# A Mamba layer with experts on one Trainium2 core: a ring of sixteen state halves, sums two steps later, and two products moved to GpSimd

## The chip, the core and the metric

The kernel runs on one core of a Trainium2 chip. TensorE multiplies matrices, VectorE (DVE) runs the scan, ScalarE (ACT) the exponentials and copies, GpSimd (POOL) elementwise products and indirect DMAs, SyncE (SP) issues the other DMAs. Each engine takes its instructions in the order of its own program; semaphores tie them together. The metric is the device time of one execution in microseconds.

## The reference

The input x has 8 batches of 512 tokens with 128 features. It is normalised; on the result work a bidirectional Mamba block and a layer of 8 experts, and both are added to x. All is float32. For each direction of Mamba (256 channels, 16 states each):

```
xi    = silu(conv4(x @ in_w.T) + conv_b)        z = x @ in_w.T (second half)
dt, B, C = split(xi @ x_w.T)                     # 8, 16, 16
delta = softplus(dt @ dt_w.T + dt_b)             A = -exp(A_log)
h[t]  = h[t-1] * exp(delta[t] * A) + delta[t] * xi[t] * B[t]
y[t]  = sum over the states of h[t] * C[t]       # per channel
out   = ((y + xi * D) * silu(z)) @ out_w.T
```

The backward direction runs over the reversed sequence. Both outputs are joined and go through combine_w; the residual is added. The experts choose one of 8 by the largest router logit for each token and compute `down(silu(gate) * up)`.

## The kernel before

A **unit** is one batch in one direction; there are 16 (two per batch, forward even, backward odd). A unit's 256 channels times 16 states are laid out as 16 **steps** of a state half of 128 partitions x 1024 numbers (32 channels x 4 groups of states on the partitions, 2 states x 512 times in the free dimension). So there are 256 steps of the scan and 32 **half batches** i of eight steps each (the two halves of a unit's channels). All five engine programs are loops over the same step number m (`for m in range(STEPS)`), and each engine does at step m, in the order in which its loop lists them, what the functions `fronts`, `tiles_at`, `gathers`, `out_step` and so on put there.

For a step m of the scan:
- TensorE spreads delta*u over the partitions (`spread_du`, L589, tile in_b), one matmul for a pair of steps, in the odd step before it;
- VectorE multiplies it by B (`du_B`, L1131), two steps at once in the even step; ScalarE makes the decay exp(delta*A) (`decay`, L947, tile dA, ring of 4), two steps ahead, from delta_rep, which SyncE copies from tmpA (`load_pair`);
- VectorE scans (`scan`, L1148 forward, L1150 backward) into hs, in the odd step; hs is a ring of NH = 13 state halves;
- GpSimd multiplies hs by C in place (L1360); for the steps in `C_ON_DVE` = 41, 56, 180, 217, 226, 255 VectorE does it (`times_C`, L1157);
- TensorE sums the states into bank Y (`sum_states`, L623): for half batch i the even halves at step 8i+12, the odd halves at 8i+13, each a set of eight matmuls that waits for the last product of its four steps. A scan that reuses a half waits for the sum that read it.

After half batch i: Y is copied to yg (`next_y`, L930, ScalarE) and multiplied by silu(z) (the **gate**, L1343, GpSimd) at step 8i+14; half batches 3, 4, 5 and 31 have their gate on VectorE (L1168). TensorE opens Y for the next half batch with xi*D (`skip`, L614) at step 8i+8. The projection out of a batch (`out_mm`, L667) waits for the gates; it runs in bank F, on top of the bias (`bias_mm`, L635) and the residual (`residual_mm`, L642), at step 32b+42 to 32b+44 for all batches but the last.

The front part of the next units (in projection, x and dt projection, softplus) is woven in between. GpSimd makes delta and delta*u of a unit (`delta_du`, L1302 and L1307) some seven steps before it starts. Bank F passes from one user to the next: `bias_mm` waits for the copy of z of unit 2b+3 (`keep_z`, L882, ScalarE), and that copy, which overwrites zs, waits for the gate of the same buffer two units earlier (`wait_gated`, half batch 2(v-2)+h).

From step 33 on GpSimd also scatters the tokens to their experts by indirect DMA (L1371, 32 of them), from step 208 on it gathers the experts' results (L1333, L1336, four at a time, in steps 208, 212 and so on up to 236); in a step's program they stand ahead of the gate. The experts run between on TensorE and ScalarE.

Of the kernel before, what the change touches and what calls it, by code (L numbers as in the profile page):

```python
# [21 lines left out]
NSTEP = J * R // RH  # L22
UNITS = 2 * NB
# [3 lines left out]
EPS = 1e-5  # L27
LAST = UNITS * NSTEP
NP, NR = 3, 5
NA, NH = 4, 13  # L30
LEAD = 2
LATE = 2
CLEAR = 3
# [2 lines left out]
NW, ND = 2, 2  # L36
SILU_SET, EXP_SET = "silu_and_others", "natural_log_exp_and_others"
GATE_ON_DVE = (3, 4, 5, 2 * UNITS - 1)
C_ON_DVE = (41, 56, 180, 217, 226, LAST - 1)

C_ID, C_TRI, C_SEL, C_IOTA, C_THR, C_NOTFIRST, C_TILE = 0, 128, 256, 288, 296, 328, 584
C_SPREAD = C_TILE + NTILE
# [55 lines left out]
def out_step(b, k):  # L98


    s0 = NSTEP * (2 * b + 1)
    if b < NB - 1:
        return s0 + NSTEP + (12, 12, 12, 12, 10, 13, 13, 12)[k]
    return s0 + (8, 9, 17, 21, 4, 22, 25, 17)[k]


STEPS = max(LAST + 6, out_step(NB - 1, 6) + 1, gather_step(NB - 1) + 10)
# [25 lines left out]
def mamba_moe_kernel(nc, x, in_wT, conv_wT, x_wT, dt_wT, A_log, out_w, comb_wT, comb_b,  # L133
                     col_vectors, router_wT, gate_up, down, consts, out):
    ctx = ExitStack()
    with ctx:
# [365 lines left out]
        def tensor_program(e):  # L502
# [192 lines left out]
            for m in range(STEPS):  # L695
                u, s = divmod(m, NSTEP)
                for i in range(1, 2 * UNITS):
                    if 8 * i + 8 == m:
                        skip(i)
                if m == 0:  # L700
                    z_proj(0, 0)
# [9 lines left out]
                    in_proj(v, 1, 0)  # L711
                for v in fronts(m, -13, -13):
                    in_proj(v, 1, 1)
                if m >= 12 and m - 12 < LAST - 8 and (m - 12) % 8 == 0:
                    u2, s2 = divmod(m - 12, NSTEP)
                    sum_states(u2, s2 // 8, 0)
                for v in fronts(m, -10, -11):
                    x_proj(v)
                for b in turns(m, -18):
# [40 lines left out]
                for b in gathers(m, 7):  # L760
                    if b < NB - LATE:
                        final_mm(b)
                if m >= 13 and m - 13 < LAST - 8 and (m - 13) % 8 == 0:
                    u2, s2 = divmod(m - 13, NSTEP)
                    sum_states(u2, s2 // 8, 1)
                for b in range(NB):
                    if out_step(b, 4) == m:
                        bias_mm(b)
# [36 lines left out]
        def scalar_program(e):  # L805
# [118 lines left out]
            def next_y(i):  # L924

                u, h = divmod(i, 2)
                e.wait_ge(pe_y, 2 * i + 2)
                if u >= 2:
                    e.wait_ge(pe_out, i - 3)
                e.copy(yg[:, u % 2, h, :], Y[:, :]).then_inc(act_y, 1)  # L930
# [55 lines left out]
            for m in range(STEPS):  # L986
# [75 lines left out]
                for v in fronts(m, -8, -9):  # L1062
                    table(EXP_SET)
                    softplus(v, 0)
                if m % 8 == 6 and m >= 8:
                    if m // 8 - 1 not in GATE_ON_DVE:
                        next_y(m // 8 - 1)
                for b in range(NB):
                    if out_step(b, 5) == m:
                        e.wait_ge(pe_out, 4 * b + 4)  # L1070
# [16 lines left out]
        def vector_program(e):  # L1087
# [191 lines left out]
            for m in range(STEPS):  # L1279
                u, s = divmod(m, NSTEP)  # L1280
                for i in GATE_ON_DVE:
                    if m == (LAST + 5 if i == 2 * UNITS - 1 else 8 * i + 15):
                        gate(i)
                for i in range(2):
                    if m >= R0:
                        route(2 * (m - R0) + i)
                    if m < LAST and m % 2 == 0:
                        du_B(m + i)
                    elif m < LAST:
                        scan(m - 1 + i)  # L1290
                for x in C_ON_DVE:
                    if m % 2 and x in (m - 1, m):
                        times_C(x)
# [3 lines left out]
        def gpsimd_program(e):  # L1297
# [17 lines left out]
            for m in range(STEPS):  # L1315
                u, s = divmod(m, NSTEP)
                for b in gathers(m, 2):
                    i = b - (NB - LATE)
                    if b == 0:
                        e.wait_ge(out_ys[0], 16 * (NTILE + 1) // 2)  # L1320
                        e.wait_ge(out_ys[1], 16 * (NTILE // 2))
                    if i < 0:
                        if b >= 2:
                            e.wait_ge(pe_fin, b - 1)
                    elif i == 0:
                        e.wait_ge(out_xn, 16 * NB)
                        e.wait_ge(pe_xn_turned, NB)
                    else:
                        e.wait_ge(out_fin[0], 16 * (NB - LATE) // 2)
                    for k in range(KB):  # L1330
                        at = bass.IndirectOffsetOnAxis(ap=pos_u[:, b * KB + k:b * KB + k + 1], axis=0)
                        if i < 0:
                            e.indirect_dma_start(out=rows_of(b)[:, k, :], out_offset=None, in_=ffn_d,  # L1333
                                                 in_offset=at).then_inc(in_gather[b % 2], 16)
                        else:
                            e.indirect_dma_start(out=late_in[i][:, k, :], out_offset=None, in_=ffn_d,  # L1336
                                                 in_offset=at).then_inc(in_late[i], 16)
                if m % 8 == 6 and m >= 8 and m // 8 - 1 not in GATE_ON_DVE:
                    i = m // 8 - 1
                    k = (slice(None), i // 2 % 2, i % 2, slice(None))  # L1340
                    e.wait_ge(act_y, gates_on_pool(i))
                    e.wait_ge(act_zs, i + 1)
                    e.tensor_tensor(yg[k], yg[k], zs[k], ALU.mult).then_inc(pool_gated, 1)  # L1343
                for n in [n - 1 for n in tiles_at(m, 11) if n % 2] + gates_at(m, 12):
                    e.wait_ge(act_up, n + 1)
                    if n == NTILE - 1:
                        e.wait_ge(act_gate, NTILE)
                    else:
                        e.wait_ge(act_thf, n // 2 * 2 + 2)
                    e.tensor_tensor(th_f[:, n % 3, :], th_f[:, n % 3, :], up_f[:, n % 2, :],  # L1350
                                    ALU.mult).then_inc(pool_acted, 1)
                for h in range(2):
                    for v in fronts(m, (-7, -4)[h], (-8, -6)[h]):
                        delta_du(v, h)
                if m < LAST and m not in C_ON_DVE:
                    p, rh, jj = place(s)
                    e.wait_ge(dve_scan, m + 1)
                    if s == 0:
                        wait_bc(e, u)
                    e.tensor_tensor(hs[:, m % NH, :], hs[:, m % NH, :],  # L1360
                                    C_rep[:, u % 2, RH * rh:RH * rh + RH, :].rearrange("p r t -> p (r t)"),
                                    ALU.mult).then_inc(pool_C, 1)
                for c in range(NB):
                    for k in range(KB):
                        if R0 + 6 + (20 * c + 5 * k) // 8 == m:
                            if k == 0:
                                e.wait_ge(in_sort[c % 2], 16 * (c // 2 + 1))
                            if c == 0 and k == 0:
                                e.wait_ge(dve_route, N_POS)
                                e.wait_ge(out_clear, 160)  # L1370
                            e.indirect_dma_start(  # L1371
                                out=sorted_d, out_offset=bass.IndirectOffsetOnAxis(
                                    ap=pos_u[:, c * KB + k:c * KB + k + 1], axis=0),
                                in_=attn_in[:, c % 2, k, :], in_offset=None).then_inc(out_sort[c % 2], 16)
# [71 lines left out]
```

## Time and profile before

| | |
|---|---|
| median of 3 runs | 923.8 us (922.23 to 923.9) |
| span of the profiled execution | 921.1 us, 2.7 less than the median |
| VectorE busy | 882.0 us, 96% |
| GpSimd busy | 801.1 us, 87% |
| TensorE matmuls busy | 736.6 us, 80% |
| ScalarE busy | 699.8 us, 76% |
| products with C on GpSimd | 250, 585.5 us |
| scans | 256, 570.4 us |

A span runs from the first to the last instruction of the profile. A row of a timeline has the start, the duration, the engine, the line, the operation, out<-in and, in brackets, the idle time before it with what ended it. Durations of one instruction in a group are means in ns. Neighbouring instructions of an engine overlap by some 0.1 us at their ends.

### The profile page before, as it was taken

What the parts mean: (1) busy time and instruction counts of PE and PEld (TensorE: products, weight loads), DVE (VectorE), ACT (ScalarE), POOL (GpSimd) and SP (SyncE); (2) the same over time, 40 slices, a digit from 0 to 9 for tenths busy, and PEclk for the clock granted to TensorE, in tenths of its full rate; (3) what the DMA queues carried; (4) which work ended last, traced back from release to release, by engine and by line L of the source; (5) the groups of instructions that cost most, each with busy time, mean ns of one, the idle gap of its engine ahead of it and who ended that gap; (6) DMA issues with size and microseconds to landing.
All of it is one profiled execution on the core that took longest, in us unless ns stands there. A gap on an engine that the chain in (4) does not pass through costs nothing. (4 is left out here: it accounts for less than half of the span.)

```text
span 921.1 us, 10735 instructions
## 1 busy us (share of the span) xinstructions
PE 736.6 (80%) x3033; PEld 327.7 (36%) x3033; DVE 882.0 (96%) x631; ACT 699.8 (76%) x1183; POOL 801.1 (87%) x450
## 2 busy tenths in 40 slices
PE   8678877777488978979788987979786987878377
PEld 5233322231134534444343534436332431323022
DVE  5899999999899999999999999999999999999986
ACT  5798876646569789888989889998979776585531
POOL 1578786999999989998799898999798989999994
PEclk9978789788698999999999999989999799879578
DMA  7875342343265546445365636455554345553300
GB/s 229 224 221 144 109 111 58 139 100 101 110 162 158 152 154 175 138 136 149 134 151 177 156 84 209 124 185 125 181 140 134 85 95 163 108 170 75 85 0 12
DMA packets 87227, 123.45 MB, mean 134 GB/s; under 512 B 7929, under 2 KB 58490, under 8 KB 83202
## 3 DMA queue, kind: packets, MB, share of 16 engines
q1 hardware_dynamic: 85122, 118.58, 46.5%
q0 software_dynamic: 2048, 4.20, 1.5%
q8 instruction: 25, 0.41, 0.2%
q14 instruction: 32, 0.26, 0.1%
HBM read 75.44 MB, written 14.29 MB: 97 GB/s over the span
## 5 line engine op out<-in xcount | busy, mean ns | idle before, releaser
L1360 POOL TENSOR_TENSOR hs<-hs,C_rep 128x1024 f32<-128x1024 f32 x250 | 585.5, 2362 | 52.1 <-DVE hs L1150 27.8
L947 ACT ACTIVATE dA<-delta_rep,A_sb 128x511 f32<-128x511 f32 x512 | 338.2, 717 | 92.8 <-DVE hs L1150 47.1
L1131 DVE TENSOR_TENSOR in_b<-in_b,B_rep 128x1024 f32<-128x1024 f32 x256 | 300.1, 1216 | 15.7 <-PE in_b L589 14.7
L1150 DVE TENSOR_TENSOR_SCAN hs<-dA,in_b 128x1024 f32<-128x1024 f32 x128 | 285.3, 2267 | 5.3 <-PE y L623 5.3
L1148 DVE TENSOR_TENSOR_SCAN hs<-dA,in_b 128x1024 f32<-128x1024 f32 x128 | 285.1, 2267 | 1.4 <-PE y L623 1.4
L589 PE MATMUL in_b<-du,cst 128*128 128x512 f32 x256 | 160.8, 714 | 57.3 <-DVE hs L1150 43.6
L623 PE MATMUL y<-hs,cst 128*32 128x512 f32 x1024 | 139.5, 652 | 21.9 <-POOL hs L1360 21.9
L550 PE MATMUL front<-xpad,w_in 128*128 128x512 f32 x248 | 119.3, 616 | 9.0 <-ACT xi L876 7.3
L956 ACT ACT_TABLE_LOAD x71 | 91.1, 1283 | 8.3 <-PE moe L733 3.7
L589 PEld LDWEIGHTS in_b<-du,cst 128*128 128x128 f32 x256 | 46.8, 214 | 134.4 <-issue 132.6
L623 PEld LDWEIGHTS y<-hs,cst 128*32 128x32 f32 x1024 | 29.6, 116 | 113.8 <-issue 71.0
L550 PEld LDWEIGHTS front<-xpad,w_in 128*128 128x128 f32 x248 | 46.3, 197 | 66.0 <-issue 48.3
L582 PE MATMUL front<-tmpB,w_dt 8*128 8x512 f32 x62 | 40.1, 730 | 25.5 <-ACT tmpB L909 16.7
L564 PE MATMUL front<-xpad,w_in 128*128 128x512 f32 x62 | 38.8, 711 | 15.9 <-ACT tmpB L912 8.6
L1302 POOL TENSOR_TENSOR tmpA<-tmpA,tmpB 128x512 f32<-128x512 f32 x31 | 39.5, 1276 | 12.9 <-ACT tmpB L922 12.8
L733 PEld LDWEIGHTS moe<-xsT,gu_w 128*128 128x128 f32 x234 | 32.7, 202 | 35.2 <-issue 35.2
L614 PE MATMUL y<-xi,diag_D 128*128 128x512 f32 x62 | 39.4, 723 | 5.3 <-ACT yg L930 4.3
L1343 POOL TENSOR_TENSOR yg<-yg,zs 128x512 f32<-128x512 f32 x28 | 35.6, 1270 | 9.1 <-ACT yg L930 9.1
L751 PEld LDWEIGHTS moe<-dn_w,th_f 128*128 128x128 f32 x234 | 33.7, 205 | 26.9 <-issue 18.4
L733 PE MATMUL moe<-xsT,gu_w 128*128 128x128 f32 x234 | 35.7, 291 | 9.4 <-ACT ys L1019 5.6
L1307 POOL TENSOR_TENSOR du<-tmpA,xi 128x512 f32<-128x512 f32 x31 | 39.5, 1273 | 2.4
L1371 POOL DMA_INDIRECT sorted_tokens<-attn_in,pos_u x32 | 33.4, 1045 | 8.9 <-issue 8.8
(147 smaller groups left out, 803.0 us busy)
## 6 DMA issues: line engine op xcount, KB each, us to landing
delta_rep<-tmpA SPq DMA_DIRECT2D x126, 256.0 KB, 3.9
C_rep<-dbc_scratch SPq DMA_DIRECT2D x16, 1024.0 KB, 7.2
B_rep<-dbc_scratch SPq DMA_DIRECT2D x15, 1024.0 KB, 5.0
gu_w<-in_gate_up SPq DMA_DIRECT2D x39, 384.0 KB, 3.8
dn_w<-in_down SPq DMA_DIRECT2D x39, 192.0 KB, 2.6
xs<-sorted_tokens SPq DMA_DIRECT2D x39, 64.0 KB, 3.9
sorted_ffn<-ys SPq DMA_DIRECT2D x39, 64.0 KB, 2.4
sorted_tokens<-up_f SPq DMA_DIRECT2D x9, 256.0 KB, 4.5
```

Source lines behind the costliest of these rows:

```text
L550: i = e.matmul((M if v == 0 and h else F)[:, :], w_in[:, d, k, h * P:(h + 1) * P], xpad[:, at:at + L], start=(k == 0), stop=(k == NTAP - 1))
L582: e.matmul((M if v == 0 and h else F)[:, :], w_dt[:, d, h * P:(h + 1) * P], dbc[0:DR, :], start=True, stop=True).then_inc(pe_dt, 1)
L589: e.matmul(in_b[:, 2 + 2 * (j % 2), :], spread(j), du[:, du_slot(v, j // 4), :], start=True, stop=True).then_inc(pe_du, 1)
L623: i = e.matmul(Y[c * DD:(c + 1) * DD, :], sel, hs[:, (m + 2 * c + rh) % NH, r * L:(r + 1) * L], start=False, stop=(rh == 1 and r == RH - 1 ...
L733: i = e.matmul(M[:, c * P:(c + 1) * P], gu_w[:, w, 0, c * P:(c + 1) * P], xsT[:, n % 2, :], start=True, stop=True)
L947: i = e.activation(dA[:, m % NA, r * L + 1:(r + 1) * L], src, ACT.Exp, scale=A_sb[:, d, 2 * p + jj, RH * rh + r:RH * rh + r + 1])
L956: e.preload_act_table_set(name)
L1131: e.tensor_tensor(to, in_b[:, 2 + 2 * odd, :].unsqueeze(1).broadcast_to([P, RH, L]), by, ALU.mult).then_inc(dve_mult, 1)
L1148: e.tensor_tensor_scan(to, a[:, 0:n], b, 0.0, ALU.mult, ALU.add).then_inc(dve_scan, 1)
L1150: e.tensor_tensor_scan(to[:, ::-1], a[:, 1:n + 1][:, ::-1], b[:, ::-1], 0.0, ALU.mult, ALU.add).then_inc(dve_scan, 1)
L1302: e.tensor_tensor(tmpA[:, h, :], tmpA[:, h, :], tmpB[:, h, :], ALU.add).then_inc(pool_delta, 1)
L1360: e.tensor_tensor(hs[:, m % NH, :], hs[:, m % NH, :], C_rep[:, u % 2, RH * rh:RH * rh + RH, :].rearrange("p r t -> p (r t)"), ALU.mult).th ...
```

## The change

Six edits. The ring hs has 16 state halves, made possible by a smaller scratch for the descriptors of GpSimd's DMAs, 4096 bytes of each partition. The sums of half batch i are at step 8i+14 and 8i+15 (for the half batch 30 at 8i+12 and 8i+13 as before). The copy of Y and the gate on GpSimd are at step 8i+16, on VectorE at 8i+17 (half batch 31 as before). skip of half batch i is at 8i+10, of half batch 31 as before. The products with C of steps 41 and 56 are on GpSimd. The steps of all other work stay.

```
-NA, NH = 4, 13
+NA, NH = 4, 16
-C_ON_DVE = (41, 56, 180, 217, 226, LAST - 1)
+C_ON_DVE = (180, 217, 226, LAST - 1)
+def sum_step(i, rh):
+    return 8 * i + rh + (14 if i < 2 * UNITS - 2 else 12)
+def y_step(i):
+    return sum_step(i, 0) + 2
+def skip_step(i):
+    return y_step(i - 1) + 2
+def halves_at(step, m):
+    return [i for i in range(2 * UNITS - 1) if step(i) == m]
 # TensorE
-                    if 8 * i + 8 == m:
+                    if skip_step(i) == m:
                         skip(i)
-                if m >= 12 and m - 12 < LAST - 8 and (m - 12) % 8 == 0:
-                    u2, s2 = divmod(m - 12, NSTEP)
-                    sum_states(u2, s2 // 8, 0)
+                for i in range(2 * UNITS - 1):
+                    if sum_step(i, 0) == m:
+                        sum_states(i // 2, i % 2, 0)
 # (the odd halves, at m - 13, in the same way with sum_step(i, 1))
 # ScalarE
-                if m % 8 == 6 and m >= 8:
-                    if m // 8 - 1 not in GATE_ON_DVE:
-                        next_y(m // 8 - 1)
+                for i in halves_at(y_step, m):
+                    if i not in GATE_ON_DVE:
+                        next_y(i)
 # VectorE
-                    if m == (LAST + 5 if i == 2 * UNITS - 1 else 8 * i + 15):
+                    if m == (LAST + 5 if i == 2 * UNITS - 1 else y_step(i) + 1):
                         gate(i)
 # GpSimd
-                if m % 8 == 6 and m >= 8 and m // 8 - 1 not in GATE_ON_DVE:
-                    i = m // 8 - 1
+                for i in halves_at(y_step, m):
+                    if i in GATE_ON_DVE:
+                        continue
-    nc = bacc.Bacc("TRN2", target_bir_lowering=False, num_devices=1)
+    nc = bacc.Bacc("TRN2", target_bir_lowering=False, num_devices=1,
+                   dynamic_dma_scratch_size=4096)
```

## Rows read from the trace of the kernel before

**Rows 1.** Busy time by stretch; columns: stretch, length, engines with counts, TensorE clock, DMA share.

```profile
157.00:326.00 169.00, 131.56 (x507) 54.59 (x511) 164.08 (x101) 116.48 (x197) 161.17 (x96) 0.85 0.45 127
326.00:744.00 418.00, 354.23 (x1680) 175.78 (x1670) 414.79 (x252) 369.82 (x634) 382.63 (x207) 0.95 0.53 147
744.00:897.00 153.00, 109.33 (x364) 37.86 (x362) 146.50 (x90) 94.11 (x146) 143.46 (x88) 0.83 0.38 99
```

**Rows 2.** Costliest groups, VectorE: busy us, mean ns of one, idle before with releaser.

```profile
L1131 DVE TENSOR_TENSOR in_b<-in_b,B_rep 128x1024 f32<-128x1024 f32 x256 | 300.1, 1216 | 15.7 <-PE in_b L589 14.7 <-DMA B_rep<-dbc_scratch 0.8
L1157 DVE TENSOR_TENSOR hs<-hs,C_rep 128x1024 f32<-128x1024 f32 x6 | 9.2, 1530 | 0.1
```

**Rows 3.** Costliest groups, GpSimd.

```profile
L1360 POOL TENSOR_TENSOR hs<-hs,C_rep 128x1024 f32<-128x1024 f32 x250 | 585.5, 2362 | 52.1 <-DVE hs L1150 27.8 <-DVE hs L1148 23.5
```

**Rows 4.** Timeline of VectorE, its products with C of steps 41 and 56.

```profile
179.04 3.05 DVE L1157 TENSOR_TENSOR hs<-hs,C_rep 128x1024 f32<-128x1024 f32 x1
...
236.17 1.19 DVE L1157 TENSOR_TENSOR hs<-hs,C_rep 128x1024 f32<-128x1024 f32 x1
```

**Rows 5.** Timeline of GpSimd beside these two, and delta of unit 4.

```profile
181.16 1.81 POOL L1371 DMA_INDIRECT sorted_tokens<-attn_in,pos_u  x1 [0.17 <-issue]
...
236.39 1.84 POOL L1371 DMA_INDIRECT sorted_tokens<-attn_in,pos_u  x1 [0.17 <-issue]
238.54 0.96 POOL L1371 DMA_INDIRECT sorted_tokens<-attn_in,pos_u  x1 [0.30 <-issue]
...
249.99 1.26 POOL L1302 TENSOR_TENSOR tmpA<-tmpA,tmpB 128x512 f32<-128x512 f32 x1
```

**Rows 6.** Timeline of TensorE, steps 60 to 76 (x counts weight loads too).

```profile
247.78 3.64 PE L623 MATMUL y<-hs,cst 128*32 128x512 f32 x16 [10.30 <-POOL hs L1360]
...
294.36 1.71 PE L635 MATMUL front<-comb_bias,ones 1*128 1x512 f32 x2
...
299.70 2.83 PE L623 MATMUL y<-hs,cst 128*32 128x512 f32 x16
```

**Rows 7.** Timeline of VectorE, steps 61 to 64, and step 78.

```profile
251.49 2.29 DVE L1150 TENSOR_TENSOR_SCAN hs<-dA,in_b 128x1024 f32<-128x1024 f32 x1 [3.05 <-PE y L623]
253.69 2.34 DVE L1131 TENSOR_TENSOR in_b<-in_b,B_rep 128x1024 f32<-128x1024 f32 x2
...
260.31 2.33 DVE L1131 TENSOR_TENSOR in_b<-in_b,B_rep 128x1024 f32<-128x1024 f32 x2
...
308.54 2.36 DVE L1131 TENSOR_TENSOR in_b<-in_b,B_rep 128x1024 f32<-128x1024 f32 x2 [1.83 <-PE in_b L589]
```

**Rows 8.** Timeline of ScalarE, the decay of step 64.

```profile
256.27 1.33 ACT L947 ACTIVATE dA<-delta_rep,A_sb 128x511 f32<-128x511 f32 x2 [10.91 <-DMA delta_rep<-tmpA]
```

**Rows 9.** Timeline of GpSimd, delta of unit 5 at step 72.

```profile
294.22 1.28 POOL L1302 TENSOR_TENSOR tmpA<-tmpA,tmpB 128x512 f32<-128x512 f32 x1
```

**Rows 10.** Waits of VectorE between 326 and 744 us: total us, times, longest.

```profile
DVE in_b L1131 <- PE in_b L589: 2.7, 3, 1.3
DVE hs L1148 <- PE y L623: 0.5, 2, 0.3
```

**Rows 11.** Timeline of GpSimd, gates of half batches 24 and 27, delta of unit 15.

```profile
739.67 1.26 POOL L1343 TENSOR_TENSOR yg<-yg,zs 128x512 f32<-128x512 f32 x1 [0.60 <-ACT yg L930]
...
830.97 1.26 POOL L1343 TENSOR_TENSOR yg<-yg,zs 128x512 f32<-128x512 f32 x1
...
841.75 1.28 POOL L1302 TENSOR_TENSOR tmpA<-tmpA,tmpB 128x512 f32<-128x512 f32 x1
```

**Rows 12.** Timeline of ScalarE, the copy of z of unit 15.

```profile
832.32 0.59 ACT L882 COPY zs<-front 128x512 f32<-128x512 f32 x1 [1.56 <-POOL yg L1343]
```

**Rows 13.** Timeline of TensorE, steps 234 to 237.

```profile
832.95 1.12 PE L635 MATMUL front<-comb_bias,ones 1*128 1x512 f32 x2 [2.39 <-ACT zs L882]
...
837.62 1.92 PE L623 MATMUL y<-hs,cst 128*32 128x512 f32 x16
...
840.43 3.73 PE L667 MATMUL front<-w_out,yg 128*128 128x128 f32 x32
844.00 1.02 PE L589 MATMUL in_b<-du,cst 128*128 128x512 f32 x2
```

**Rows 14.** Timeline of VectorE, step 246.

```profile
878.65 2.37 DVE L1131 TENSOR_TENSOR in_b<-in_b,B_rep 128x1024 f32<-128x1024 f32 x2 [3.35 <-PE in_b L589]
```

More of the change, by code:

```diff
@@ L762, in tensor_program @@
                         final_mm(b)
-                if m >= 13 and m - 13 < LAST - 8 and (m - 13) % 8 == 0:
-                    u2, s2 = divmod(m - 13, NSTEP)
-                    sum_states(u2, s2 // 8, 1)
+                for i in range(2 * UNITS - 1):
+                    if sum_step(i, 1) == m:
+                        sum_states(i // 2, i % 2, 1)
                 for b in range(NB):
```

## The prediction

> **What bounds the kernel now.** I read four views, in this order: busy time by stretch, the costliest groups of each engine, the timelines of the engines around every idle piece of VectorE, and who waited for whom. The first shows three stretches after the routing has begun: VectorE is busy for 164.1 of 169 us, 414.8 of 418 and 146.5 of 153 [rows 1]. So the scan of VectorE is the bound, and all it can still give is its idle time and what is taken off it. But GpSimd is nearly as full in the first and third stretch (161.2 of 169, 143.5 of 153), while in the second it idles for 35.4 us. VectorE's own waits for TensorE's in_b come to 14.7 us in the whole run, and its six products with C to 9.2 [rows 2]. One of its products with C takes 2362 ns [rows 3], and a pair of steps on VectorE has a period of 260.31 - 253.69 = 6.62 us [rows 7], so GpSimd falls behind when scatters, gathers or gates come on top. Most of VectorE's longer stalls come from that lag.
>
> I number steps as the code does (step m, state half m, i the half batch of eight steps). By counting, the scan at 251.49 is that of step 61, the products of VectorE at 179.04 and 236.17 are those of steps 41 and 56.
>
> **1. Two products leave VectorE (steps 41, 56).** They took 3.05 and 1.19 us there [rows 4]: 4.24 us, all on VectorE's own path. On GpSimd they cost 2 x 2.36 = 4.72 us [rows 3]. Beside each of them an indirect DMA of GpSimd took 1.81 and 1.84 us, with 0.96 for its undisturbed neighbour [rows 5]; I take these 2 x 0.86 = 1.7 us back, so GpSimd is 3.0 us later from step 57 on (bounds: 3.0 and 4.7). [...]
>
> **2. Sixteen halves and sums two steps later.** The scan of step 61 stood 3.05 us until the sum of half batch 6 was done, after a TensorE wait of 10.30 us for GpSimd [rows 6, 7]. With the new ring, the scan may run ten steps ahead of the product instead of seven, so this stall goes. Together with part 1 VectorE would be 4.24 + 3.05 = 7.3 us earlier at step 64. What is late next is also on GpSimd: delta and D*u of unit 4, which stand in its queue at step 57, behind both added products. delta ended at 249.99 + 1.26 = 251.25 [rows 5]; its copy was there 5.0 us later, and ScalarE's decay of step 64, 1.33 us, began at 256.27 [rows 8]. Moved by 3.0 us that ends at 260.6, where the scan of step 64 stood at about 260.31 + 2.25 = 262.6 [rows 7]. So **only 2.0 us of the 7.3 are left at step 64.**
>
> **3. The gate two steps later, first place (steps 72 to 78).** Moving the gate of half batch 7 from step 70 to 72 puts it behind two more products on GpSimd. Its user is ScalarE's copy of z of unit 5, at step 74, which may overwrite zs only then; behind this copy TensorE waits with the bias of batch 1 in the same bank, and behind that with the next two in_b. The product of step 71, with the gate ahead of it, ended at 294.27 (the next GpSimd instruction starts at 294.22 [rows 9]); the order of the two is exchanged, the sum is the same, so the gate now ends at 294.3 + 3.0 = 297.3. The copy takes 0.59, as the one of unit 15 [rows 12], and the bias starts at 297.9 instead of 294.36 [rows 6]. From that start to the first work of VectorE at step 78 it was 308.54 - 294.36 = 14.2 us [rows 6, 7], of which a sum of 2.83 us moves behind step 78: 11.3 us. Step 78 thus starts at 309.2, with 308.54 before. Some of the matmuls after the sum will run at the lower clock, which adds up to 1: I take **+1.0 us** here (bounds -3.8, if the wait is hidden: 2.0 + the stall of 1.83 [rows 7]; and +2.4, by the 4.7 of part 1).
>
> **4. The middle.** GpSimd catches up here: 35.4 us of idle time [rows 1] against 3. The gate waits are hidden while its lag is small. VectorE's idle time in this stretch is 2.7 us in three pieces behind in_b, and 0.5 in two behind a sum [rows 10]. The 0.5 go with the ring. Of the 2.7 one piece stands behind a sum and a projection out in the same step, as at step 78, and goes; the others stand behind a wait for ScalarE, where the moved sum now fills TensorE's gap. I take **-2.1 us** in all (bounds 0 and -3.2). skip (D*u) at its new step stands directly ahead of the copy that frees xi; the four matmuls after it have a pair's time, so nothing is added.
>
> **5. The gate two steps later, second place (steps 208 to 246).** GpSimd works nearly without a break (143.5 of 153 us [rows 1]). A gate at step 206 ran at 739.67 in front of an idle piece [rows 11]; moved to 208 it lies inside the full stretch, +1.26. The gate of half batch 27 ran at 830.97 at step 230 and released ScalarE's copy of z of unit 15 at 832.32 (its wait is named: GpSimd's yg), and this released TensorE's bias at 832.95 after 2.39 us [rows 11 to 13]. At step 232 it stands behind two more products and, since gathers are issued first in a step, **behind four indirect DMAs**: all that ended at 841.75, where delta of unit 15 starts [rows 11]. Gate 24 has come into the stretch where gate 27 has left it, so gate 27 itself ends at 841.75 + 1.26 = 843.0, and the bias starts at 832.95 + 10.8 = 843.75. From the bias to the end of the second in_b behind it (844.00 + 1.02 = 845.02) it was 12.07 us, less the sum of 1.92 that moves away [rows 13], plus about 1 for a colder start: 11.2. So step 78's picture returns at step 238: in_b is ready at 854.9. VectorE then needs four periods to step 246: 854.9 + 26.5 = 881.4, where it stood at 878.65 after a stall of 3.35 [rows 14]. That stall and the one of the ring before it are gone, but the same time and more is lost earlier: **+2.75 us**. From there nothing new waits, and the end follows VectorE. The floor, if TensorE is in time, is set by GpSimd with the one more gate: 1.26 less some 0.6 of idle time, +0.7.
> [...]
>
> **6. The smaller DMA scratch.** No row of before shows its filling. A scatter takes 0.96 to 1.84 us [rows 5] and names no wait for an earlier one; I take 0. If it were too small, a DMA in a group of four would wait for the one before to land. The nearest row is the 5.0 us from tmpA's end to the landed copy, so 3 of 4 in each of 16 groups would wait about 5 - 1.3 = 3.7 us: +180 us on a full engine. Below nothing there is no reason for a gain. [...]
>
> **Sum.** 0 (start) + 1.0 - 2.1 + 2.75 = +1.65 us on the span of 921.1. The median is 923.8, 2.7 over the span, which I keep: 921.1 + 1.65 + 2.7 = 925.5 us.
>
> **Rivals.**
> A. Both z copies are hidden: TensorE or ScalarE reach them later than I think. Then part 3 is -3.8, part 4 -2.1, part 5 +0.7: -5.2, 918.6 us. For it: VectorE's gains are plain in the rows. Against it: rows 12 and 13 show the copy of unit 15 waiting for the gate already.
> B. One of the two bites: -3.8 - 2.1 + 2.75 = -3.2, 920.6; or 1.0 - 2.1 + 0.7 = -0.4, 923.4.
> [...]
> D. The change does not do what it says, the ring being held by the scratch: far over 950.
>
> **How the numbers follow.** Forecast 0.47; A 0.16; B 0.19; C 0.15, mostly its half; D 0.01; 0.02 for others. The predicted time is the forecast's. The range reaches to A below and between the half and the whole of C above: 918.5 to 931. A measurement tells about 0.2% here, 1.85 us: faster is under 921.95, slower over 925.65. The forecast with its own spread of 922 to 928 gives 0.24 to slower, 0.21 to same and 0.02 to faster; A is faster; B is 0.09 faster and 0.10 same; C, D slower. Together: faster 0.27, same 0.32, slower 0.41.
>
> **What would show it.** Right: the copy of z before step 76 and, most of all, the last one, at about 843.6, waits for GpSimd's yg; VectorE stalls at in_b of steps 76, 236 and 238 and no longer at the scans of steps 61, 238 and 245; the decay of step 64 waits for its copy; VectorE keeps four products with C. Wrong: in_b of step 238 ready near 845 (A); the projection out of step 236 over 5 us (C); idle pieces of over 1 us between GpSimd's gathers (D).

## The result and the profile after

The changed kernel takes 972.2 us in the median of 5 runs (965.9 to 975.4), the kernel before beside it 923.9: a ratio of 1.050, with a 95% interval of 1.048 to 1.053. The prediction said 925.5 us with a range of 918.5 to 931. The profiled execution took 965.9 us, the least of the five, with a span of 963.8, so 42.7 us more than the 921.1 of before; the medians lie 48.3 us apart. What follows reads the 42.7 us of the spans, each of one execution.

The head of the page, span and busy time of each engine:

```profile
span 963.8 us, 10692 instructions
PE 749.1 (78%) x3033; PEld 330.1 (34%) x3033; DVE 879.9 (91%) x629; ACT 698.8 (73%) x1183; POOL 803.5 (83%) x452
```

VectorE does 2.1 us less work (882.0 before) and idles 44.8 us more: 83.9 instead of 39.1. TensorE is busy for 12.5 us more with the same 3033 matmuls, at a mean granted clock of 0.888 instead of 0.897. Who waited for whom, selected rows: total us, times, longest:

```profile
DVE in_b L1148 <- PE in_b L606: 60.8, 27, 10.2
POOL yg L1361 <- ACT yg L947: 56.4, 10, 9.9
...
ACT xi L893 <- issue: 22.4, 12, 4.1
...
PE front L590 <- ACT xi L906: 20.1, 6, 4.2
...
ACT tmpA L928 <- PE front L599: 18.0, 7, 3.7
...
DVE hs L1165 <- PE y L640: 0.6, 1, 0.6
```

The same waits in the kernel before, in its own line numbers:

```profile
DVE in_b L1131 <- PE in_b L589: 14.7, 11, 3.4
...
POOL yg L1343 <- ACT yg L930: 9.1, 6, 3.2
...
PE front L573 <- ACT xi L889: 8.6, 6, 2.1
...
ACT tmpA L911 <- PE front L582: 4.4, 4, 1.9
```

VectorE's wait behind in_b has grown by 46.1 us and the one behind a sum has fallen by 6.1, from 6.7 to 0.6: the ring did what it was meant to do, and TensorE was late in its place. GpSimd's 56.4 us of waiting for the copy of Y look like the cause, and for the most part are not (the copy of Y first, below). The busy time by stretch shows where. The last three stretches hold about the same steps as those of [rows 1]; they start later, since the changed kernel is late by then, and the first stands for the 157 us ahead of [rows 1]:

```profile
0.00:167.00 167.00, 124.13 (x405) 53.95 (x406) 139.85 (x181) 116.09 (x204) 100.97 (x56) 0.86 0.54 150
167.00:340.00 173.00, 132.64 (x517) 52.81 (x515) 162.97 (x101) 117.20 (x200) 165.54 (x99) 0.87 0.44 124
340.00:782.00 442.00, 364.60 (x1680) 179.54 (x1680) 412.98 (x250) 368.18 (x630) 377.76 (x206) 0.93 0.50 140
782.00:940.00 158.00, 112.89 (x363) 38.49 (x362) 147.53 (x91) 94.36 (x147) 147.07 (x89) 0.82 0.35 94
```

And the start of the kernel before:

```profile
0.00:157.00 157.00, 125.00 (x422) 53.95 (x422) 139.77 (x181) 116.06 (x204) 101.39 (x56) 0.88 0.57 160
```

VectorE's idle time is 27.2 us in the start (17.2 before), 10.0 in the next stretch (4.9), **29.0 in the middle (3.2)** and 10.5 in the last (6.5). The middle is where I had expected GpSimd's slack to hide everything, and the start is where I had expected nothing at all. By step, from the ends of the scans in both timelines, the changed kernel is later by 0.8 us at step 19, 10.2 at 31, 9.6 at 39, 5.4 at 63, 11.5 at 79, 18.1 at 95, 24.8 at 127, 31.0 at 159, 38.6 at 175 to 223, 48.5 at 239 and 42.7 at 255. So ten microseconds go before the scatters begin, and in the middle the loss comes in small portions once or twice a unit.

**One such portion.** The timeline of the changed kernel around steps 86 to 90 (start, duration, engine, line):

```profile
344.64 1.62 PE L750 MATMUL moe<-xsT,gu_w 128*128 128x128 f32 x6 [3.40 <-DMA gu_w<-in_gate_up]
...
346.41 3.64 PE L640 MATMUL y<-hs,cst 128*32 128x512 f32 x16
349.98 1.92 PE L590 MATMUL front<-xi,w_x 128*40 128x512 f32 x4
351.94 0.58 ACT L915 COPY tmpB<-front 40x512 f32<-40x512 f32 x1 [4.35 <-PE front L590]
...
356.02 1.92 PE L640 MATMUL y<-hs,cst 128*32 128x512 f32 x16
357.87 1.12 PE L599 MATMUL front<-tmpB,w_dt 8*128 8x512 f32 x2
359.03 0.69 ACT L928 ACTIVATE tmpA<-front,cols 128x512 f32<-128x512 f32 x1 [2.94 <-PE front L599]
...
361.09 1.62 PE L750 MATMUL moe<-xsT,gu_w 128*128 128x128 f32 x6 [2.09 <-ACT ys L1036]
362.71 1.92 PE L581 MATMUL front<-xpad,w_in 128*128 128x512 f32 x2
...
364.42 1.91 PE L606 MATMUL in_b<-du,cst 128*128 128x512 f32 x2
364.96 1.26 POOL L1361 TENSOR_TENSOR yg<-yg,zs 128x512 f32<-128x512 f32 x1 [9.17 <-ACT yg L947]
366.37 2.36 DVE L1148 TENSOR_TENSOR in_b<-in_b,B_rep 128x1024 f32<-128x1024 f32 x2 [4.86 <-PE in_b L606]
```

The same work in the kernel before:

```profile
332.48 1.92 PE L623 MATMUL y<-hs,cst 128*32 128x512 f32 x16
334.33 1.91 PE L573 MATMUL front<-xi,w_x 128*40 128x512 f32 x4
336.28 0.58 ACT L898 COPY tmpB<-front 40x512 f32<-40x512 f32 x1 [1.79 <-PE front L573]
...
341.51 0.69 ACT L911 ACTIVATE tmpA<-front,cols 128x512 f32<-128x512 f32 x1 [0.60 <-PE front L582]
...
343.57 0.91 PE L733 MATMUL moe<-xsT,gu_w 128*128 128x128 f32 x6 [1.04 <-ACT ys L1019]
...
344.42 1.02 PE L564 MATMUL front<-xpad,w_in 128*128 128x512 f32 x2
345.29 1.02 PE L589 MATMUL in_b<-du,cst 128*128 128x512 f32 x2
```

The front part of a unit passes to and fro between TensorE and ScalarE in bank F: x projection, copy, dt projection, copies, z projection, each waiting for the other engine. From the start of the x projection to the start of the in_b behind the z projection it was 345.29 - 334.33 = 11.0 us, and is 364.42 - 349.98 = 14.4. A sum stood directly ahead of that chain before, too (332.48), but the other sum of the half batch had been done 7 us earlier; now it stands inside the chain, at 356.02, ahead of the second dt projection, and takes 1.92 us there. ScalarE stands for it (2.94 instead of 0.60), its copies for the experts queue behind, TensorE stands for those (2.09 instead of 1.04), and only then comes in_b. VectorE waits 4.86 us. GpSimd's 9.17 us end at the same time, but the copy of Y that it waits for was itself late. A further part of this portion isn't the sum's place: TensorE waited 3.40 us for an expert's weights at 344.64 (1.79 at 331.53 before), and after it the sum ahead of the chain ran at a granted clock of 0.50 and took 3.64 us, instead of 1.92 at 1.00. ScalarE's 4.35 us instead of 1.79, and 1.55 us of VectorE one pair earlier, stand behind that. Why these weights were later I haven't shown.

### The profile page after: what moved, and what is told of

It is laid out like the page before. It is cut to its first block and busy times, and to the rows that moved or that the text cites. A ratio compares the mean times of both kernels' runs of the same rounds, so it can differ in the third digit from the quotient of the medians.

```text
span 963.8 us, 10692 instructions
## 1 busy us (share of the span) xinstructions
PE 749.1 (78%) x3033; PEld 330.1 (34%) x3033; DVE 879.9 (91%) x629; ACT 698.8 (73%) x1183; POOL 803.5 (83%) x452
## 5 line engine op out<-in xcount | busy, mean ns | idle before, releaser
L1148 DVE TENSOR_TENSOR in_b<-in_b,B_rep 128x1024 f32<-128x1024 f32 x256 | 300.6, 1218 | 61.8 <-PE in_b L606 60.8
L606 PE MATMUL in_b<-du,cst 128*128 128x512 f32 x256 | 158.6, 706 | 49.5 <-DVE hs L1167 36.0
L640 PE MATMUL y<-hs,cst 128*32 128x512 f32 x1024 | 145.4, 677 | 3.1 <-POOL hs L1378 3.1
L567 PE MATMUL front<-xpad,w_in 128*128 128x512 f32 x248 | 119.3, 615 | 14.7 <-ACT xi L893 13.1
L1361 POOL TENSOR_TENSOR yg<-yg,zs 128x512 f32<-128x512 f32 x28 | 35.6, 1271 | 56.5 <-ACT yg L947 56.4
L581 PE MATMUL front<-xpad,w_in 128*128 128x512 f32 x62 | 41.5, 758 | 25.0 <-ACT tmpB L929 13.2
L590 PE MATMUL front<-xi,w_x 128*40 128x512 f32 x64 | 40.2, 762 | 20.1 <-ACT xi L906 20.1
L599 PE MATMUL front<-tmpB,w_dt 8*128 8x512 f32 x62 | 37.2, 680 | 19.6 <-ACT tmpB L915 11.4
L768 PE MATMUL moe<-dn_w,th_f 128*128 128x128 f32 x234 | 35.0, 288 | 15.6 <-ACT th_f L1053 8.7
```

Of the source, the lines that this page charges most:

```text
L567: i = e.matmul((M if v == 0 and h else F)[:, :], w_in[:, d, k, h * P:(h + 1) * P], xpad[:, at:at + L], start=(k == 0), stop=(k == NTAP - 1))
L606: e.matmul(in_b[:, 2 + 2 * (j % 2), :], spread(j), du[:, du_slot(v, j // 4), :], start=True, stop=True).then_inc(pe_du, 1)
L640: i = e.matmul(Y[c * DD:(c + 1) * DD, :], sel, hs[:, (m + 2 * c + rh) % NH, r * L:(r + 1) * L], start=False, stop=(rh == 1 and r == RH - 1 ...
L768: i = e.matmul(M[:, IFP:IFP + H], th_f[:, (n - 2) % 3, c * P:(c + 1) * P], dn_w[:, (n - 2) % ND, c, :], start=(c == 0), stop=(c == NCH - 1))
L1148: e.tensor_tensor(to, in_b[:, 2 + 2 * odd, :].unsqueeze(1).broadcast_to([P, RH, L]), by, ALU.mult).then_inc(dve_mult, 1)
```

## Experiments

All the kernels compute the whole reference. Each ratio is to the kernel before on the same chip; line numbers are those of the changed kernel unless said.

### The change taken apart

**The ring alone** (NH = 16 and the scratch; steps and C_ON_DVE as before).

```
-NA, NH = 4, 13
+NA, NH = 4, 16
+                   dynamic_dma_scratch_size=4096)
```

> Only the ring of 16 halves and the smaller scratch; every step and both products as before. Theory Y (the later copy of Y, gate and skip cost the time): 918 to 924 us, the scan of step 61 waits for no sum. Theory S (the later sums push the projections of the front part): the same, 918 to 924. Theory P (two more products on GpSimd): the same. Theory R (the smaller scratch slows the indirect DMAs): 945 or more, with waits between the scatters.

Measured: 927.1 us, ratio 1.0034 (1.0014 to 1.0054), above the 918 to 924 that three of the four theories gave, and far below the 945 of the fourth. Its timeline at steps 60 to 62, in the line numbers of before:

```profile
248.70 3.64 PE L623 MATMUL y<-hs,cst 128*32 128x512 f32 x16 [9.35 <-POOL hs L1360]
252.28 1.73 PE L589 MATMUL in_b<-du,cst 128*128 128x512 f32 x2
...
254.04 2.36 DVE L1131 TENSOR_TENSOR in_b<-in_b,B_rep 128x1024 f32<-128x1024 f32 x2 [2.50 <-PE in_b L589]
```

The stall of 3.05 us at the scan of step 61 [rows 7] is gone, and one step later VectorE waits 2.50 us for in_b, which stands on TensorE behind the very sum that the scan no longer waits for. At step 246 it waits 3.9. So a longer ring frees VectorE from the sum only where nothing that VectorE needs is queued behind it.

**Ring and the two products.**

```
+C_ON_DVE = (180, 217, 226, LAST - 1)
```

> As e1_ring, and the products with C of steps 41 and 56 on GpSimd; all steps as before. Theory P: 940 or more. Theories Y and S: within 4 us of e1_ring, since delta of unit 4 on GpSimd is next late after 4.2 us taken off VectorE: 917 to 926.

Measured: 928.6 us, ratio 1.0050 (1.0026 to 1.0073), 1.5 us over the ring alone. VectorE gains 3.1 us at step 41 and loses it at in_b of steps 54 (1.6), 62 (6.0) and 66 (1.4): its waits behind in_b are 27.3 us instead of 21.5. What GpSimd got later comes back through the sum and through D*u.

**Ring, and y, gate and skip two steps later**, sums and products as before.

```
+def sum_step(i, rh): return 8 * i + rh + 12
+def y_step(i): return 8 * i + (16 if i < 2 * UNITS - 2 else 14)
+C_ON_DVE = (41, 56, 180, 217, 226, LAST - 1)
```

> Ring of 16; the copy of Y and the gate at step 8i+16, skip at 8i+10, and the sums where they were, at 8i+12 and 8i+13; products with C as before. Theory Y: 955 to 970, with the copies of xi waiting for skip and the gates on GpSimd idling for the copy of Y. Theory S: under 930.

Measured: 947.6 us, ratio 1.0243 (1.0208 to 1.0277), 20.4 us over the ring alone and between the ranges of the two theories. Here too ScalarE waits 23.8 us ahead of the copies of xi, and VectorE 10.2 at step 236. By step it is later than the kernel before by 2.7 us at step 31, 3.4 at 79, 18.8 at 223, 30.3 at 239 and 24.5 at 255.

**All steps moved, products as before** (the changed kernel with C_ON_DVE of before).

> The changed kernel with the products with C of steps 41 and 56 back on VectorE: sums, Y, gate and skip all two steps later. Theory Y: 965 to 975, within 8 us of e3_y_late. Theory S: over 955, and 25 us or more above e3_y_late. Theory P: under 940.

Measured: 973.7 us, ratio 1.0533 (1.0502 to 1.0564), 1.5 us over the changed kernel, and by step 9.2 us later than the kernel before at step 31, 9.5 at 79 and 43.8 at 223. So the two products on GpSimd are not the cause. By these four runs the ring costs 3 us, the late y, gate and skip 20, the late sums some 26, and the two products between -1.5 and +1.5.

### Three remedies, alone and together

**The gate ahead of the gathers** in GpSimd's step (the block of L1355 to L1361 stands before the indirect DMAs).

> The changed kernel with the gate ahead of the gathers in GpSimd's step (steps 208 to 236). Theory G (gate 27 behind four gathers holds the copy of z of unit 15, TensorE's bias and in_b of step 236, 10.2 us of VectorE's idle time): the stall at step 236 falls by the 4.9 us of the gathers to about 5, and since 5.8 us of it were given back later by stalls that were gone, the time falls by 3 to 5 us from the changed kernel's 972. Rival (TensorE is late there for another reason): within 1 us of it.

Measured: 967.7 us, ratio 1.0461 (1.0431 to 1.0491). VectorE's stall at step 236 is 5.33 us, with 1.10 at the next pair, where the changed kernel has 10.23. So the place behind the gathers makes about 4 us of it; the rest stays with the gate two steps late.

**Three buffers of xi**, so that its copy no longer waits for skip; NH = 15 makes the room.

```
-                if v >= 2:
-                    e.wait_ge(pe_skip, 2 * (v - 2) + 2)
+                if v >= 3:
+                    e.wait_ge(pe_skip, 2 * (v - 3) + 2)
```

> The changed kernel with three buffers for xi instead of two (and 15 state halves instead of 16, for the room), so that the copy of xi into a buffer no longer waits for the moved skip. Theory K (the later skip holds this copy, and with it the whole chain of bank F: 22.4 us of ScalarE's waits): 950 to 962. Theory S (the chain is held by the sums ahead of x and dt projection): 968 to 974.

Measured: 964.6 us, ratio 1.0432 (1.0384 to 1.0479). This lies between the two theories: the copy is a part of the cause. ScalarE's 22.4 us of waiting are gone, and VectorE's wait behind in_b falls from 60.8 to 45.9 us. The stall of step 20 shows the chain (changed kernel):

```profile
93.20 1.24 PE L631 MATMUL y<-xi,diag_D 128*128 128x512 f32 x2
94.53 0.69 ACT L893 ACTIVATE xi<-front,cols 128x512 f32<-128x512 f32 x1 [1.05 <-issue]
95.27 3.78 PE L567 MATMUL front<-xpad,w_in 128*128 128x512 f32 x4 [0.83 <-ACT xi L893]
...
102.00 1.02 PE L606 MATMUL in_b<-du,cst 128*128 128x512 f32 x2
...
103.06 1.23 DVE L1148 TENSOR_TENSOR in_b<-in_b,B_rep 128x1024 f32<-128x1024 f32 x1 [4.61 <-PE in_b L606]
```

skip releases the copy that frees bank F for the next in projection, and in_b is behind it. The copy is late by 1.05 us and TensorE by 0.83; the in projection then runs at a granted clock of 0.50 and takes 3.78 us, where its four rows took 1.88 at 88.13, at 1.00. So the stall of 4.61 isn't all of the skip. It is 2.0 us in the run with all steps moved, and none of over 0.9 us stands there in the runs with the gate or the copy of Y first, which keep the late skip.

**The sums at the end of TensorE's step**, behind the front part and in_b of that step (and a wait for D*u of the unit before in one ScalarE copy, to keep the buffers apart).

> The changed kernel with the sums at the end of their TensorE step, behind x and dt projection, in the same steps. (ScalarE's second dt copy waits for D*u of the unit before, which the order gave it until now.) Theory S: 945 to 955, TensorE's x projection no longer two microseconds late and the copies of Y on ScalarE as early as before. Theory K: 968 to 974.

Measured: 980.3 us, ratio 1.0592 (1.0546 to 1.0638), VectorE's wait behind in_b 74.4 us. This missed: it is worse than the changed kernel. A sum at the end of one step is still ahead of the next step's work: in the place read above it stands ahead of in_b (353.17 to 355.02 us) and VectorE waits 3.42. So another order within the same steps does not mend it; how much of the 8 us more is of the added wait I haven't shown.

**The copy of Y first in ScalarE's step**, ahead of dt copies and softplus.

> The changed kernel with the copy of Y at the start of ScalarE's step 8i+16 instead of its end. Theory Y2 (the copy stands behind dt copies, table loads and softplus of that step, the gate on GpSimd idles for it 56 us, and everything on GpSimd behind the gate is late): GpSimd's idle time before the gate falls under 20 us, the time by 10 to 20 us. Rival (the idle time of GpSimd is covered by its slack, and TensorE's lateness is what counts): 968 to 976.

Measured: 968.7 us, ratio 1.0469 (1.0428 to 1.0511). Two of its waits:

```profile
DVE in_b L1148 <- PE in_b L606: 60.1, 29, 9.0
POOL yg L1361 <- ACT yg L947: 24.2, 7, 4.7
```

GpSimd's wait for the copy of Y falls by 32 us, VectorE's wait behind in_b by 0.7. So most of GpSimd's 56.4 us was slack.

**The three together** (gate ahead of gathers, three xi, copy of Y first; NH = 15).

> Three changes together on the changed kernel: gate ahead of the gathers, three buffers for xi (15 state halves), copy of Y at the start of its step. If the three causes add up (4, 7 and 3 us singly): 956 to 961. If they are one chain seen from three sides: 950 to 956, more than the sum. If each only uncovers the next: over 961.

Measured: 952.4 us, ratio 1.0308 (1.0289 to 1.0326): 2.0% less than the changed kernel, where the three alone give 0.43% + 0.72% + 0.35% = 1.5%; with intervals of 0.3 to 0.5% the two can't be told apart. What is left of VectorE's wait behind in_b is 39.2 us in 23 pieces of at most 3.8. From step 16 on, 22 of VectorE's idle places are over 0.9 us, and 15 of them are at steps 16v + 8 to 16v + 12 (24, 58, 88, 90, 106, 120 and so on; v counts the units): behind the steps 16v + 5 to 16v + 9, in which TensorE has the x, dt and z projections of the next unit.

### The sums

**Sums of the odd half batches back at their old steps** (8i+12 and 8i+13, those that were moved to 16v+6 and 16v+7; everything else as in the changed kernel).

> The changed kernel with the sums of the odd half batches back at 8i+12 and 8i+13 (they had moved to the ten and nine steps before a unit's start, where x and dt projection of that unit stand); copy of Y, gate, skip and the sums of the even half batches stay late. Theory S2 (these sums add their time to the chain of x and dt projection): 948 to 954, nearly all of the 26 us between e3_y_late and e4_steps. Rival (the even ones, next to the in projection, matter): 966 to 974.

Measured: 959.4 us, ratio 1.0386 (1.0337 to 1.0434), between the two ranges expected.

**Those of the even half batches back** (moved to 16v+14 and 16v+15).

> The mirror of e10_odd_old: the sums of the even half batches are back at 8i+12 and 8i+13, those of the odd ones stay at 8i+14 and 8i+15. Theory S2: 966 to 974. Rival: 948 to 954. If both matter, each of the two kernels is near 960.

Measured: 964.3 us, ratio 1.0446 (1.0413 to 1.0479). The odd ones give back 1.2% and the even ones 0.6%, together 17 us of the 26. The odd ones share their steps with the x, dt and z projections, the even ones don't; why these cost too, and why the two halves give back less than the whole, I haven't shown.

**The three remedies and all sums at the old steps**, products as before.

```
+def sum_step(i, rh): return 8 * i + rh + 12
+def y_step(i): return 8 * i + (16 if i < 2 * UNITS - 2 else 14)
```

> The kernel of e9_three (ring of 15, three xi buffers, gate ahead of the gathers, copy of Y at the start of ScalarE's step, y, gate and skip two steps late) with all sums back at 8i+12 and 8i+13 and the products of steps 41 and 56 back on VectorE. It closes the account. If the late sums alone make up what e9_three still loses (28.5 us over before) and the three remedies have paid for the late y, gate and skip, the time is 924 to 930 us, with VectorE's waits behind in_b under 25 us. If the late y, gate and skip still cost something of their own that the remedies don't touch (the place of skip in TensorE's order), it is 932 to 942.

Measured: 925.5 us, ratio 1.0002 (0.9984 to 1.0020), and

```profile
DVE in_b L1148 <- PE in_b L606: 19.3, 12, 4.0
```

In the totals this closes the account. A late y, gate and skip with their remedies cost nothing against before; without them, and with 16 halves, it is the run of ring and late y, 2.4% slower. The late sums (with the two products) cost the whole of what the three remedies left: 1.0308 - 1.0002 = 3.1%, 28 us.

### What is left

**The late steps only where the ring had a stall** (half batches 6 and 29, ring of 16, products as before).

```
+def sum_step(i, rh): return 8 * i + rh + (14 if i in (6, 29) else 12)
+def y_step(i): return 8 * i + (16 if i in (6, 29) else 14)
```

> Ring of 16 with both products on VectorE and the later steps for half batches 6 and 29 alone, where the kernel before waited for a sum. If only the general move costs time: the stalls of steps 61 and 245 and 246 go and nothing takes their place in the middle, 915 to 921 us, faster than the kernel before. If moving even two half batches costs as much as it gives: 924 to 930.

Measured: 928.8 us, ratio 1.0042 (1.0016 to 1.0067). It missed. The stalls at 61, 62, 245 and 246 are all gone; at step 63 it is 2.1 us ahead of the kernel before. Then comes

```profile
269.21 2.36 DVE L1148 TENSOR_TENSOR in_b<-in_b,B_rep 128x1024 f32<-128x1024 f32 x2 [4.33 <-PE in_b L606]
```

at step 66, 1.5 at step 72 and 5.0 at step 252. A stall that is taken away where GpSimd is full comes back at the next point where VectorE meets it.

**The scratch alone** (the kernel before with the smaller scratch, ring of 13).

> The kernel before with the smaller scratch for DMA descriptors alone, ring of 13 and all steps as before. It splits the 3 us that the ring and the scratch cost together (927.1 against 923.9). Theory ring: the scratch costs nothing, as its indirect DMAs keep their 0.96 to 1.0 us and name no new wait: 923 to 925 us, stall of 3.05 us at step 61 as before. Theory scratch: the 3 us come from it, 926 to 928 us, with longer indirect DMAs or idle time ahead of them on GpSimd.

Measured: 925.0 us, ratio 0.9998 (0.9981 to 1.0015). The indirect DMAs keep their mean (32 scatters of 1047 ns, with 1045 before) and the stall at step 61 its 3.1 us. So if the 3 us of the ring's run are real (its interval begins at 0.1%), they are of the ring, and not of the scratch. The profile of the ring alone shows only 0.8 us of span; it is of one of its faster executions, 923.9 us, and of the rest no row tells.

**VectorE's product at another step** (the kernel before with 40 in place of 41).

```
-C_ON_DVE = (41, 56, 180, 217, 226, LAST - 1)
+C_ON_DVE = (40, 56, 180, 217, 226, LAST - 1)
```

> The kernel before with VectorE's product of step 41 exchanged for that of step 40. The one of step 41 began at 179.04 beside GpSimd's product, which ran until 181.00, and ended at 182.09, 1.09 us after it, which is the time of a whole undisturbed product (1.19). Theory lock: VectorE's product with two SBUF inputs stands still while a product of GpSimd runs; at step 40 GpSimd's product has ended (176.18) before VectorE's begins (176.83), so it takes 1.2 us, 1.85 less, while the indirect DMA beside it becomes 0.9 longer: VectorE is 1.9 us earlier at step 44, and 921.5 to 924 us at the end, as some of it is lost at step 61. Rival: the 3.05 us belong to something else at that place (the refilling of C_rep, for one), and the product of step 40 takes as long or the time doesn't move: 923.5 to 925.

Measured: 925.2 us, ratio 0.9997 (0.9977 to 1.0016). No gain, because I had the order wrong: VectorE does its product of an even step only behind the pair of scans, so it meets GpSimd's next product again. Its timeline (lines of before):

```profile
181.90 2.35 POOL L1360 TENSOR_TENSOR hs<-hs,C_rep 128x1024 f32<-128x1024 f32 x1
182.18 3.16 DVE L1157 TENSOR_TENSOR hs<-hs,C_rep 128x1024 f32<-128x1024 f32 x1
184.41 1.81 POOL L1371 DMA_INDIRECT sorted_tokens<-attn_in,pos_u  x1 [0.17 <-issue]
```

But it repeats the measurement. GpSimd's product ends at 184.25 and VectorE's at 185.34, 1.09 later; in the kernel before they ended at 181.00 and 182.09, again 1.09 apart. An undisturbed one takes 1.19 [rows 4], so in both cases VectorE's product seems to have done its work only once GpSimd's had ended, and the DMA beside it took 1.81 instead of 0.96 us. The changed kernel has a third case at step 217: VectorE's product began at 815.28 beside one of GpSimd's that ended at 815.92, and ended at 817.01, 1.09 later.

## Why the prediction was wrong, by its steps

**The sum's first term, "0 (start)", failed.** It stands there without a working: I read no row ahead of 157 us, though the sums, the copy of Y, the gate and skip move there too. The changed kernel is 0.8 us late at step 19 and 10.2 at step 31, more than all my terms together. VectorE waits 4.61 us at step 20 and 3.29 at step 24 behind in_b, and 2.32 behind ScalarE's copy of the router logits. With y, gate and skip late alone it is 2.7 us at step 31, with all steps moved 9.2, so most of it is of the late sums.

**Part 4 failed, in two sentences.** The first is on skip: "stands directly ahead of the copy that frees xi; the four matmuls after it have a pair's time, so nothing is added". I looked at how long the matmuls had, and not at who else waits in that chain. The rows show the copy of xi waiting 12 times, 22.4 us in all, then the in projection for the copy, and in_b behind both; with three buffers of xi, which take the wait for skip away, the 22.4 us are gone and VectorE's wait is down by 14.9 us. The second is "the moved sum now fills TensorE's gap", and with it the -2.1 us for the middle. TensorE's gaps that I have read there are not free time: they are waits for ScalarE inside the chain of bank F, and a sum of 1.9 us (3.64 at a granted clock of 0.50) that starts in a gap ends after it. The sums of the odd half batches had their old steps at 16v+4 and +5, ahead of the second dt projection and of z; at 16v+6 and +7 they stand in among them. (In the backward units, whose x projection is at 16v+5, one had stood inside the chain before, too.) I read only the VectorE side of the move. The late sums cost 26 to 28 us over the whole kernel by the runs. From step 79 to step 223 the changed kernel loses 27.3 us, where I had -2.1 with nothing for skip; with y, gate and skip late alone it is some 15 us there, so both sentences have a large share.

**Part 5 was right in its mechanism and 1.2 us too small.** The last gate stands behind four gathers, as predicted; ScalarE's copy of z of unit 15 waits for it:

```profile
880.88 0.94 POOL L1350 DMA_INDIRECT gu_w<-sorted_ffn,pos_u  x1 [0.30 <-issue]
881.85 1.27 POOL L1361 TENSOR_TENSOR yg<-yg,zs 128x512 f32<-128x512 f32 x1
883.21 0.58 ACT L899 COPY zs<-front 128x512 f32<-128x512 f32 x1 [11.15 <-POOL yg L1361]
883.84 2.07 PE L652 MATMUL front<-comb_bias,ones 1*128 1x512 f32 x2 [10.21 <-ACT zs L899]
...
887.96 2.36 DVE L1148 TENSOR_TENSOR in_b<-in_b,B_rep 128x1024 f32<-128x1024 f32 x2 [10.23 <-PE in_b L606]
```

TensorE stands 10.21 us (2.39 before [rows 13]) and VectorE 10.23, all of it at step 236 and none at step 238. The shift goes from 38.8 to 48.5 us there and back to 42.7 at the end, since the stalls of 2.2 and 3.4 us at steps 245 and 246 are gone. So this place costs 48.5 - 38.8 - 5.8 = 3.9 us, with +2.75 forecast.

The microsecond that parts 3 and 5 add for a lower clock was my estimate, and no run shows it by itself. In its place the runs showed this: at step 236 it was 894.84 - 883.84 = 11.00 us from the bias to the end of the second in_b, with 12.07 - 1.92 = 10.15 before, and the bias took 2.07 us at a granted clock of 0.50 instead of 1.12 at 1.00; at step 78 the same stretch took 9.96 us, all at 1.00.

**Part 2 held, by another path.** The scan of step 61 no longer waits, and delta and D*u of unit 4 are late next. delta begins 13.1 us later than before, where the kernel was 9.56 late at step 39: 3.6 us are of GpSimd, between my bounds of 3.0 and 4.7. Then comes D*u:

```profile
264.46 1.26 POOL L1324 TENSOR_TENSOR du<-tmpA,xi 128x512 f32<-128x512 f32 x1
265.78 2.08 PE L606 MATMUL in_b<-du,cst 128*128 128x512 f32 x2 [3.94 <-POOL du L1324]
267.89 2.36 DVE L1148 TENSOR_TENSOR in_b<-in_b,B_rep 128x1024 f32<-128x1024 f32 x2 [2.13 <-PE in_b L606]
269.37 1.33 ACT L964 ACTIVATE dA<-delta_rep,A_sb 128x511 f32<-128x511 f32 x2 [15.47 <-DMA delta_rep<-tmpA]
```

Through the copy for the decay, as I had it, it costs 0.5 us of VectorE's time; through in_b, which I had not named, 2.13. At the scan of step 64 the kernel is 8.24 us late, so 1.3 of the 7.3 us are left, with 2.0 forecast.

**Part 3 missed the other way at its own place.** The gate of half batch 7 ran at 306.10, and ScalarE's copy of z followed it at 307.45, as said. But from the bias at 308.55 to the end of the second in_b took 10.0 us, where I had 11.3 to VectorE's start: at step 78 VectorE did not wait at all, and its old stall of 1.83 is gone. The projection out took 3.74 us, at a granted clock of 1.00. But VectorE had waited 2.51 us at step 58, 2.79 at step 66 and 1.89 at step 70 behind in_b, which parts 1 to 3 do not have. From step 39 to 79 the three parts come to +1.9 us, with +1.0 forecast: that the two are near is luck.

**Part 1** gave 3.1 us at step 41, as read. **Part 6** was right: the scratch costs nothing that the runs can tell (0.9998, 0.9981 to 1.0015). With the scratch alone no scatter names a wait for an earlier one to land: their idle time is 8.7 us in all, put down to issue, with 8.8 before, and at most 2.0 in one piece in both.

**The rivals.** C had the clock still low at the projection out. How much that adds was estimated from the ratio of 3.64 to 1.92 us, and the upper end of the range came from it. It shows once: at step 174 TensorE waited 4.01 us for a DMA of the experts' weights, the projection behind it took 5.80 us at a granted clock of 0.63 instead of 3.73 at 1.00, and VectorE stood 6.08. At step 236, the place that I had named for it, the projection took 3.73 us, at 1.00. So it is not the reason for the loss. None of the rivals held the mechanism that decided: moved work that lands in steps where two other engines alternate.

**What I could have read.** The waits of before list 8.6 us of TensorE's x projection behind ScalarE, 4.4 of ScalarE behind the dt projection and 11.7 of another behind the x projection. These are the links of a chain with little slack (at the place read above in_b was ready at 346.31 us, and VectorE took it at 348.27), and the timeline of one unit with all three engines side by side would have shown which steps are free of them. I took GpSimd's idle time as the measure of slack in the middle; it was TensorE's that was wanted.

## What to carry to other kernels

A step that is moved by two has two costs, and only one is on its own data: list what its engine does in the steps that it leaves and in those that it enters, and who waits for what stands behind it in both. A gap in an engine's timeline is free only if the instruction at its end isn't itself on the way to the bound; a gap that ends with a wait for another engine in a to-and-fro is part of a chain. A wait that one remedy shortens is worth only what the bound engine's own wait falls by: the copy of Y first took 32 us off GpSimd's waits and 0.7 off VectorE's.

## What the runs showed of the hardware

VectorE's product of hs with C (two operands in SBUF) seems to have stood still while a product of GpSimd ran that had begun before it: 3.05, 3.16 and 1.74 us beside one, 1.19 without, ending 1.09 us after GpSimd's in all three cases. Where VectorE's began first, by 0.16 us (654.39 us, kernel before), it took 1.20 and GpSimd's 3.25 instead of 2.36. GpSimd's indirect DMA took 1.79 to 1.84 us beside the rest of VectorE's, and mostly 0.96 to 1.01 without. The multiplication by B (one operand in PSUM) shows no such wait: its 256 have a mean of 1216 ns, with GpSimd 87% busy.

TensorE's matmuls of one sum (eight in the kernel; the profile has sixteen rows of MATMUL for them and counts the weight loads apart, so the x16 of [rows 6] holds no weight loads) took 1.92 us in the flow (837.62 us, kernel before) and 3.64 after a wait of 9.35 us (248.70 us, ring alone), with granted clocks of 1.00 and 0.50. The projection out took 5.80 us instead of 3.73 after a wait of 4.01 and a group of six matmuls, with 0.63 instead of 1.00. In these cases a wait in front of TensorE cost more than its length, and so it was with the sum ahead of the chain of bank F: 3.64 us at 346.41, after a wait of 3.40 and a group of six.
